# First wide attention: the zero test of two units as one VectorE operation over two neighbouring PSUM banks

## What is computed

```python
def _L0_xattn_ref(xq, xk, xv, mask, w_q, w_k, w_v, w_o, b_o):
    q = jnp.einsum('bsd,hdk->bhsk', xq, w_q)
    kk = jnp.einsum('btd,hdk->bhtk', xk, w_k)
    v = jnp.einsum('btd,hdv->bhtv', xv, w_v)
    scores = jnp.einsum('bhsk,bhtk->bhst', q, kk) / jnp.float32(d_k)
    masked = scores * mask[:, None, None, :]
    scores = jnp.where(masked == 0.0, -jnp.inf, masked)
    attn = jax.nn.softmax(scores, axis=-1)
    out = jnp.einsum('bhst,bhtv->bhsv', attn, v)
```

## Time and profile before

| | us |
|---|---|
| median of 3 runs | 546.78 |
| lowest and highest of them | 546.55, 550.07 |
| span of the profiled execution, first to last instruction | 545.7 |
| DVE busy in the span | 431.3 |
| PE busy in the span | 503.3 |

### The profile page before, as it was taken

One profiled execution on the slowest core, in us unless ns is written; L12 is line 12 of the kernel. 1 busy time (PEld: TensorE's weight loads), 2 busy tenths in 40 slices (PEclk: granted clock), 3 DMA queues, 4 the chain that ended last, 5 costly groups with the idle time before them and its releaser, 6 DMA issues. The chain is left out here.

```text
span 545.7 us, 13308 instructions
## 1 busy us (share of the span) xinstructions
PE 503.3 (92%) x4905; PEld 289.4 (53%) x4905; DVE 431.3 (79%) x1208; ACT 341.1 (63%) x683; POOL 282.0 (52%) x307
## 2 busy tenths in 40 slices
PE   7889999999899899998998899998999999999996
PEld 3345556667753233343334467635665556954574
DVE  7999999997585888736867899888777777587763
ACT  5698888888247366643762678638888888422212
POOL 7957777777834734400110943227888888400100
PEclk9999999999999899999999899999999999999999
DMA  8660000001130000000000221000000002000000
GB/s 226 141 176 14 1 2 3 1 2 41 40 117 0 2 0 2 3 1 0 2 1 21 78 78 58 2 1 1 2 3 1 1 3 79 2 0 1 2 0 20
DMA packets 24084, 15.43 MB, mean 28 GB/s; under 512 B 8083, under 2 KB 22230, under 8 KB 23894
## 3 DMA queue, kind: packets, MB, share of 16 engines
q1 hardware_dynamic: 24022, 14.60, 9.4%
HBM read 14.33 MB, written 0.26 MB: 27 GB/s over the span
## 5 line engine op out<-in xcount | busy, mean ns | idle before, releaser
L509 PE MATMUL pspair<-ident,PP 128*128 128x128 f32 x512 | 82.0, 283 | 2.0 <-ACT PP L1342 1.8
L509 PEld LDWEIGHTS pspair<-ident,PP 128*128 128x128 f32 x512 | 54.2, 141 | 29.7 <-issue 20.1
L524 PE MATMUL psO<-V,PP 128*128 128x64 f16 x1536 | 65.7, 193 | 2.6 <-DVE Oall L1751 2.0
L524 PEld LDWEIGHTS psO<-V,PP 128*128 128x128 f16 x1536 | 59.9, 98 | 9.1 <-DVE PP L1717 2.9
L1717 DVE TENSOR_TENSOR PP<-pspair,PP 128x512 f16<-128x512 f32 x64 | 44.0, 688 | 25.7 <-ACT PP L1326 25.7
L1405 ACT ACTIVATE PP<-pspair 128x1024 f32<-128x1024 f32 x48 | 46.5, 1021 | 25.4 <-PE pspair L709 25.3
L2401 POOL TENSOR_TENSOR ln_rs<-ln_ve,minus_half 128x4 f32<-128x4 f32 x10 | 10.3, 1032 | 84.2 <-DVE ln_ve L1608 81.0
L1342 ACT ACTIVATE PP<-scores_m,nm 128x512 f32<-128x512 f32 x64 | 46.5, 727 | 5.4 <-DVE nm L1701 5.4
L2412 POOL TENSOR_TENSOR PP<-acc,one 128x512 f16<-128x512 f32 x32 | 33.3, 1040 | 29.3 <-ACT acc L1324 29.3
L2412 POOL TENSOR_TENSOR PP<-y_sb,one 128x512 f16<-128x512 f32 x32 | 33.3, 1040 | 16.9 <-ACT y_sb L1324 16.9
L2415 POOL TENSOR_TENSOR PP<-y_sb,PP 128x512 f16<-128x512 f32 x32 | 37.2, 1161 | 2.5
(11 more groups left out here) (596 smaller groups left out, 1261.2 us busy)
## 6 DMA issues: line engine op xcount, KB each, us to landing
W<-in_L_ffn_W SPq DMA_DIRECT2D x16, 256.0 KB, 2.8
bigw<-in_L_xattn_w_q SPq DMA_DIRECT2D x2, 512.0 KB, 6.4
bigw<-in_L_xattn_w_kv SPq DMA_DIRECT2D x1, 1024.0 KB, 4.7
V<-in_ctx SPq DMA_DIRECT2D x1, 512.0 KB, 4.8
bigw<-in_L_xattn_w_v SPq DMA_DIRECT2D x1, 512.0 KB, 6.2
mask_b<-in_mask_BxS_ff SPq DMA_DIRECT2D x1, 512.0 KB, 7.6
bigw<-in_L_xattn_w_k SPq DMA_DIRECT2D x1, 512.0 KB, 5.8
bigw<-in_L_xattn_w_o SPq DMA_DIRECT2D x1, 512.0 KB, 3.9
```

The source lines that it names most:

```text
L509: mm = pe.transpose(bank[f"T{j % 2}"][:, k * P:(k + 1) * P], Pb[j % 4][:, k * P:(k + 1) * P], ident[:])
L524: mm = pe.matmul(bank["O"][:, (j % UPH) * a.dv:(j % UPH + 1) * a.dv], (PTH, PTL)[ppart][j % 4][:, k * P:(k + 1) * P], (VH, VL)[vpart][:, b ...
```

## The change

The score banks S0 and S1 become a third two-bank PSUM tensor, so that units 0 and 1 of four lie side by side as units 2 and 3 did before. `zeros` is called once per pair, takes both banks (128 x 1024) in one operation, writes both halves of Zt, and counts up the semaphore by 2 when it has ended. It waits for both banks to be full, and for both `stat`s of the pair before.

```diff
-        bank = {b: ctx.enter_context(nc.psum_tensor(f"ps{b}", [P, 512], F32))[:] for b in ["S0", "S1", "O", "M"]}
-        pairs = [ctx.enter_context(nc.psum_tensor(f"pspair{k}", [P, 2, 512], F32)) for k in range(2)]
-        for k, b in enumerate(["S2", "S3", "T0", "T1"]):
+        bank = {b: ctx.enter_context(nc.psum_tensor(f"ps{b}", [P, 512], F32))[:] for b in ["O", "M"]}
+        pairs = [ctx.enter_context(nc.psum_tensor(f"pspair{k}", [P, 2, 512], F32)) for k in range(3)]
+        for k, b in enumerate(["S2", "S3", "T0", "T1", "S0", "S1"]):
             bank[b] = pairs[k // 2][:, k % 2, :]
...
         zero_m = [Zt[:].bitcast(BF16)[:, k * SK:(k + 1) * SK] for k in range(2)]
+        zero_m2 = Zt[:].bitcast(BF16).rearrange("p (u s) -> p u s", u=2)
...
                 def zeros(i, j):
 
-                    ps = filled(dve, f"{n}.S{j % 4}", affine(i, j, UPI, 4))
-                    if not isinstance(i, int) or i * UPI + j >= 2:
-
-                        emptied(dve, f"{n}.S{(j - 2) % 4}", affine(i, j - 2, UPI, 4))
-                    dve.tensor_scalar(zero_m[j % 2], ps[:], 0.0, -BIG, ALU.is_equal, ALU.mult)\
-                        .then_inc(sem(f"{n}.zeros"), 1)
+                    for u in (j, j + 1):
+                        filled(dve, f"{n}.S{u % 4}", affine(i, u, UPI, 4))
+                    if i * UPI + j >= 2:
+                        for u in (j - 2, j - 1):
+                            emptied(dve, f"{n}.S{u % 4}", affine(i, u, UPI, 4))
+                    dve.tensor_scalar(zero_m2, pairs[0 if j % 4 else 2][:], 0.0, -BIG, ALU.is_equal, ALU.mult)\
+                        .then_inc(sem(f"{n}.zeros"), 2)
...
-                            for k in (3, 4) if j % 2 else ():
-                                if j + k < end:
-                                    zeros(*shift(i, j + k))
+                            if j % 2 and j + 3 < end:
+                                zeros(*shift(i, j + 3))
...
                     for j in range(0, 4, 2):
                         zeros(0, j)
-                        zeros(0, j + 1)
```

## The result

| | before | after |
|---|---|---|
| median, us | 546.71 (6 runs) | 551.37 (6 runs) |
| lowest and highest, us | 545.02, 551.54 | 549.62, 555.85 |
| span of the profiled execution, us | 545.7 | 547.9 |

The change makes the kernel slower: ratio 1.0096, 95% interval 1.006 to 1.0132. That is 4.7 us, about 1%. The forecast was 546.4 us with a range up to 549.0.

The account below looks back on a forecast made before the run. DVE was taken to bound the first wide attention. Pair savings of 0.44 + 0.60, less 0.52 and 0.11, gave 0.41 us; forecast 0.4 us less, median 546.78 to 546.4 us, range 544.3 to 549.0.

Parts of the forecast that it names:

- What bounds the stage: First wide attention, 25 to 135 us: DVE, busy 108.12 of 110 us, bounds it; other engines add 0.17 us per 13.75 us period.
- The merged test: One 128x1024 zero test on DVE lasts 1.217 us, where a pair of 128x512 tests takes 1.28 us.
- The second rival: Merged test on DVE is dearer, restarting at the bank border: 548.4 us at 1.28 us length, 551.3 at 1.37; chance 0.15.
- the length d: Duration of the merged zero test on DVE, taken as 1.217 us; from 1.230 us on the change would lose time.
- The price of a bare wait is 0.11 us: On DVE, `stat` starts 0.03 us after the test it needs, where an independent operation starts 0.08 us ahead of the end.
- bare pairs: The 11 of 32 test pairs with `stat` directly behind on DVE: 0.047 us lost each, 0.52 us in all.
- late start: DVE's test after `evac` starts 0.17 us late, behind PE's score matmuls, once per 8 units; forecast to stay.
- The wait for both banks: Where DVE waits for PE's score matmuls, also waiting for the second bank costs 0.02 us, 6 times: 0.1 us.
- The prologue: Before the rounds, the second test directly follows the `stat` of unit 1 and must wait for its end: 0.11 us lost.
- The sum is 0.41 us saved: DVE's pairs and prologue together: 0.44 + 0.60 - 0.52 - 0.11 us, before 0.1 us for the second bank.
- The loop takes it: Rival: PE, ACT or POOL wait longer for `stat`, or DVE waits longer for PE; no change, 546.8 us; chance 0.2.
- The rule named as a rival: Semaphores between DVE operations cost nothing extra; leads to the full-saving rival, 544.8 us or 542.0 us, chance 0.1.

## Why the prediction was wrong

- **What bounds the stage**: right. DVE's losses of 0.51 us per period came out as 0.52 in the period; the 0.04 us per pair that the early memset saved on DVE came through to the stage by half.
- **The merged test**: right. Forecast 1.217 us, measured 1.218; to `query_low` 1.137 and 1.13. The second rival (a dearer test) had the right side and a time of 551.3 at its far end. That this is the measured time is chance, for the mechanism is not there: the length d stayed below 1.230 us, and the loss came all the same.
- **"The price of a bare wait is 0.11 us"**: this is the step that failed. I read it at an operation that waits on the one before by a wait that it carries, and gave it to one whose blocking wait is not carried. The runs show two prices: carried, 0.03 to 0.05 us after the end (1.25 or 1.26 us from the start, forecast 1.247), and separate, 0.20 us (1.42). Against the overlap of 0.08 us that is 0.13 and 0.28. On 11 bare pairs and 14 with `recip` the difference is 25 x 0.17 = 4.3 us, most of the 5.0 us between forecast and result. Undoing it alone gave 2.66 us, since part of it then went into the late start (0.91 us behind `evac`, 0.22 behind PE). My bounds for this wait went down to no price at all and had nothing above the value itself, so the range had no room for it.
- **The wait for both banks**: "I take 0.02 us, 6 times". It failed too, by ten times at that place: 0.22 us behind PE in place of 0.03. With the wait for the second bank carried and the first bank's dropped it is 0.07 us, so the bank itself costs 0.04, twice what I took, and the two separate wait instructions 0.15. And it cost 0.10 us at the other start behind `evac`, where every bank had long been full, and where I had priced nothing. Undoing it alone gave 2.01 us, of which 0.6 are the two stops.
- **The prologue**: forecast 0.11. The two first pairs are bare, and the second test starts 0.83 us after the `stat` before it, against 0.61: 0.22.
- **"The sum is 0.41 us saved"**: the forecast of 0.4 us less leaves out the 0.1 us that I had just found for the second bank, so it should have been 0.3. That fits the kernel whose blocking waits are carried, with a stage 0.27 us shorter. The kernel that was written loses 4.37.
- **The loop takes it**: false for the most part. When DVE became faster (the wait of `stat` carried, 0.16 us at 25 places) the stage followed by 2.66 us; the late start behind PE took up some 0.16 us per period.
- **The rule named as a rival**: by the Trainium skill, page "VectorE: DVE Perf Modes", section "The DRAIN you can't avoid", a semaphore between two operations costs nothing extra. The runs don't agree, by 0.11 to 0.13 us (carried) or 0.28 us (separate) of start-to-start time.

What stays open: why a separate wait costs 0.06 us more than a carried one when PE releases it and 0.13 us more when DVE itself does (0.16 against 0.03, no memset between), why two in a row cost 0.10 us behind `evac` and nothing behind `norm`, and the two stops of DVE at 52 and 86 us.

## What to carry to other kernels

Merging two operations of an engine removes what lay between the first and its reader. Ask which wait then blocks, and look in the compiled program whether the instruction carries it. What helped here: write first the wait that will be met last, drop waits that others imply, and let counts go up by 1. A price read from one dependent pair holds only for pairs whose wait stands in the same place.

## What was unexpected of the hardware

- A wait on the operation right ahead on DVE: the next start is 0.03 to 0.05 us after its end if the wait is carried, 0.16 if it is in a separate wait instruction, 0.20 if a memset stands behind that.
- Two separate wait instructions in a row cost 0.10 us though met (0.70 against 0.60 us behind `evac`), but nothing behind `norm` (0.33 us in both); one costs nothing when met and 0.06 us when it is what PE releases.
- A 128x1024 operation over two PSUM banks takes 1.218 us where two of 128x512 take 1.28: no visible price for the second bank, and 0.06 us saved.
